# Projections in four parts, three and five per gap of a level; sums of squares' vector work in later gaps; a reordered head

## The reference

```python
qkvz = xn @ W_qkvz ; b, a = xn @ W_ba        # 16 heads of q and k, 32 of v and z, 128 wide
q, k, v = silu(causal_conv1d(qkv, 4 taps))
beta = sigmoid(b); g = -exp(A_log) * softplus(a + dt_bias)
q, k = rmsnorm(q), rmsnorm(k)                # from sums of squares over 128 channels
# chunks of 64 tokens: T = inverse(I + tril(beta k k^T * decay)), then 8 steps per sequence
# v_new = v' - k_cum @ state; out = q*exp(g) @ state + attn @ v_new; state = decayed state + k^T v_new
h = norm_w * rmsnorm(out) * silu(z)
s = h @ W_out
y = x + s * silu(ffn(xn))                    # ffn with weights looked up in a table of 16
```

## Time and profile before

| | us |
|---|---|
| three runs, median (lowest, highest) | 2787.88 (2787.59, 2792.42) |
| the profiled execution | 2787.02 |
| its span, first to last instruction | 2785.1 |
| round to round (start of `outputs`, 196.58 to 274.58) | 78.0 |
| PE busy (share of the span) | 2496.7 (90%) |
| DVE, ACT, POOL busy | 1660.4, 1492.5, 1802.1 |
| the chain that ended last, by engine | PE 68%, DVE 20%, no recorded cause 6%, the rest 6% |

### The profile page before, as it was taken

One profiled execution on the slowest core, in us unless ns is written; L12 is line 12 of the kernel. 1 busy time (PEld: TensorE's weight loads), 2 busy tenths in 40 slices (PEclk: granted clock), 3 DMA queues, 4 the chain that ended last, 5 costly groups with the idle time before them and its releaser, 6 DMA issues.

```text
span 2785.1 us, 104069 instructions
## 1 busy us (share of the span) xinstructions
PE 2496.7 (90%) x41680; PEld 1718.8 (62%) x41680; DVE 1660.4 (60%) x2967; ACT 1492.5 (54%) x3206; POOL 1802.1 (65%) x1829
## 2 busy tenths in 40 slices
PE   3599999989999998999999899999899999998799
PEld 1366666666666666666666566666666666666444
DVE  5466666666666666666666566666566666665322
ACT  1456566555556566555556566555565566554211
POOL 0576667787666666787666667787666667787100
PEclk8799999999999999999999999999999999998899
DMA  3111011111111011111111011011110111110200
GB/s 96 35 35 31 16 31 39 30 34 33 35 35 31 17 30 40 28 35 33 35 35 31 17 31 39 28 35 33 36 35 16 32 31 39 27 35 2 58 22 16
DMA packets 71100, 90.28 MB, mean 32 GB/s; under 512 B 16720, under 2 KB 39376, under 8 KB 70480
## 3 DMA queue, kind: packets, MB, share of 16 engines
q1 hardware_dynamic: 70608, 83.40, 11.7%
HBM read 78.30 MB, written 5.08 MB: 30 GB/s over the span
## 4 chain that ended last, share of the span: by engine, by line
PE 68%; DVE 20%; issue 6%; DVEq 1%; ACT 1%; DMA 0%; POOLq 0%; ACTq 0%; SPq 0%; POOL 0%
PE ps_two L406 9%; PE ps_two L582 8%; DVE XW L926 6%; PE ps_p L422 5%; PE ps_p L524 4%; PE ps_state L387 4%; PE ps_two L387 4%; PE ps_state L548 4%; DVE XW L937 4%; PE ps_p L419 3%; PE ps_p L418 3%; PE ps_p L502 3%; PE ps_two L572 3%; DVE hT L990 2%; PE ps_p L532 2%
## 5 line engine op out<-in xcount | busy, mean ns | idle before, releaser
L1072 POOL TENSOR_TENSOR Sd<-St,el 128x512 f32<-128x512 f32 x192 | 201.2, 1048 | 605.3 <-DVEq L971 500.1
L1108 POOL TENSOR_SCALAR hT<-idx_s,lutb 128x134 f32<-128x134 int32 x480 | 355.4, 744 | 27.5
L954 DVE TENSOR_SCALAR Vn<-ps_p,bR 128x128 f32<-128x128 f32 x512 | 164.6, 349 | 257.2 <-PE ps_p L497 183.6
L742 ACT ACTIVATE Xs<-XW 64x512 f32<-64x512 f32 x320 | 200.9, 628 | 207.7 <-DVE XW L937 201.5
L418 PEld LDWEIGHTS ps_p<-XW,U 64*64 64x64 f32 x5120 | 170.9, 137 | 222.3 <-issue 222.3
L857 DVE SCALAR_TENSOR_TENSOR cacc<-ps_two,cw,cacc 128x1022 f32<-128x1022 f32 (+2 forms) x192 | 243.1, 1266 | 84.2 <-ACT cacc L653 81.8
L418 PE MATMUL ps_p<-XW,U 64*64 64x64 f32 x5120 | 189.3, 223 | 112.0 <-DVE XW L926 104.2
L387 PE MATMUL ps_two<-xnT,w_qkv 128*128 128x512 f32 x512 | 258.7, 629 | 21.6 <-DVEq L862 19.8
L857 DVE SCALAR_TENSOR_TENSOR cacc<-ps_state,cw,cacc 128x1022 f32<-128x1022 f32 (+2 forms) x192 | 244.4, 1273 | 39.7 <-ACT cacc L653 18.2
L387 PE MATMUL ps_state<-xnT,w_qkv 128*128 128x512 f32 x512 | 253.3, 618 | 0.8 <-DVEq L862 0.8
L422 PEld LDWEIGHTS ps_p<-XW,P 64*64 64x64 f32 x5120 | 166.7, 136 | 132.1 <-issue 132.0
(11 more groups left out here) (156 smaller groups left out, 6115.5 us busy)
## 6 DMA issues: line engine op xcount, KB each, us to landing
qg<-g_scratch SPq DMA_DIRECT2D x64, 512.0 KB, 7.3
g_st<-g_scratch SPq DMA_DIRECT2D x64, 256.0 KB, 5.5
w_qkv<-in_wqkvz SPq DMA_DIRECT2D x16, 512.0 KB, 3.8
w_z<-in_wqkvz SPq DMA_DIRECT2D x16, 256.0 KB, 3.1
w_o<-in_wout SPq DMA_DIRECT2D x16, 256.0 KB, 2.8
idx_s<-in_idx SPq DMA_DIRECT2D x32, 67.0 KB, 1.9
fw_scratch<-looked_up SPq DMA_DIRECT2D x32, 67.0 KB, 1.9
Kg<-in_x SPq DMA_DIRECT2D x2, 1024.0 KB, 7.6
```

The costliest lines, as they stand in the source:

```text
L742: act.activation(Xs[(1 - a) * C:(2 - a) * C], X[a * C:(a + 1) * C, 1], ACT.Copy).then_inc(s["x_c"], 1)
L1072: pool.tensor_tensor(Sd[:, :, :, :], St[:, c % 2, :, :, :], el[:, R.par, :, :, c].unsqueeze(3).broadcast_to([P, BB, RATIO, P]), ALU.mult). ...
L1108: m = pool.tensor_scalar(slots[k], idx_s[:, :], float(k), lutb[:, k:k + 1], ALU.is_equal, ALU.mult)
```

## The change

`beside` cuts a projection into four parts (k = 0, 1 for columns 0 to 255, then for 256 to 511). The first gap of a level gets parts 0, 1, 2 of the level's first projection, the second gap its part 3 and all four of the next: three and five instead of four and four. DVE's `lengths` becomes three pieces: keys' copies in step 1, reciprocal and product in step 2, queries' copies in step 7, and POOL's `with_beta` goes to steps 3 and 4. In the head POOL normalises tiles 8 to 15; ACT copies every second bank of transposes; the head projections come in ahead of and between the turned gates; tap0 of kinds 0 and 1 goes first on ACT, and `decays(HEAD)` behind silu(1); SP loads the rows as soon as g is stored, and the scalars behind the second store; POOL's `lengths(HEAD)` goes behind `first_level`. Two small inputs of the head (`wba_s`, `resets`) lie in P1 instead of cacc.

```diff
--- before.py
+++ after.py
@@ -72,7 +72,7 @@
...
 IN_LAST, _ = places(bank_uses(False))
-IN_HEAD, PER_HEAD = places(spread(PROJ, (0, 1, 6, 7)) + spread(N2, (0, 1)))
+IN_HEAD, PER_HEAD = places(spread(PROJ, (6, 7, 0, 1)) + spread(N2, (2, 3)))
 def constants():
@@ -279,16 +279,23 @@
...
         sp.dma_start(w_z[:, :, :], wqkvz[:, :, bass.ds(h * HW + 4 * HD, 2 * HD)]).then_inc(s["ld_wz"], 16)
-    def load_round(h, par):
+    def load_scalars(h, par):
         b0 = par * BB
...
                          ).then_inc(s["ld_round"], 16)
...
+    def load_rows(h, par):
+        b0 = par * BB
         for a in range(RATIO):
...
             sp.dma_start(qg[:, par, :, a, :], src.broadcast_to([P, BB, S])).then_inc(s["ld_round"], 16)
...
+    def load_round(h, par):
+        load_scalars(h, par)
+        load_rows(h, par)
     def load_idx(h, par):
@@ -299,10 +306,12 @@
...
     sp.dma_start(g_dram.rearrange("b h t -> (b h) t"), gw[0]).then_inc(s["g_out"], 16)
+    sp.wait_ge(s["g_out"], 16)
+    load_rows(0, 0)
     sp.wait_ge(s["g_sc"], 8)
...
     sp.wait_ge(s["g_out"], 32)
-    load_round(0, 0)
+    load_scalars(0, 0)
     def body(R):
@@ -348,13 +357,14 @@
...
         if q >= 2:
-            pe.wait_ge(s["ln_T"], q - 1)
+            pe.wait_ge(s["ln_T"] if q % 2 == 0 else s["ln_Ta"], q // 2)
         for i in range(4):
             t, k = (q * 4 + i) // KD, (q * 4 + i) % KD
-            pe.wait_ge(s["ln_xn"], t + 1)
+            pe.wait_ge(s["ln_xn"] if t < NT // 2 else s["ln_xp"], t % (NT // 2) + 1)
             m = pe.transpose(ps[q % 2][:, i * P:(i + 1) * P], xn[t // 8][:, t % 8, k * P:(k + 1) * P], ident)
         m.then_inc(s["ln_t"], 1)
-    pe.wait_ge(s["ln_T"], NT * KD // 4)
+    pe.wait_ge(s["ln_T"], NT * KD // 8)
+    pe.wait_ge(s["ln_Ta"], NT * KD // 8)
     for j in range(2):
@@ -363,30 +373,34 @@
...
         m.then_inc(s["ba_mm"], 1)
-    for j, src in enumerate((bdup, gdup)):
+    def turn_gates(j, src):
         pe.wait_ge(s["g_dup"], j + 1)
...
         m.then_inc(s["g_tr"], 1)
-    pe.wait_ge(s["g_sc"], 8)
     pe.wait_ge(s["zeroed"], 1)
...
         return slice((par * BB + b) * S, (par * BB + b + 1) * S)
-    def proj(R, i):
+    def proj(R, i, parts=(0, 1, 2, 3)):
         par = 0 if R.head else 1 - R.par
         kind, b = i // BB, i % BB
-        if i == 0:
-            pe.wait_ge(s["ld_w"], 32 if R.head else (R.h + R.par) * 32 + 32)
-        bank, filled = wait_open(pe, R, "proj", i)
-        for k in range(KD):
-            m = pe.matmul(bank[:, :], w_qkv[:, k, kind * P:(kind + 1) * P], xnT[:, k, cols(par, b)],
+        bank, filled = ps[R.use("proj", i)[0]], full[R.use("proj", i)[0]]
+        if 0 in parts:
+            if i == 0:
+                pe.wait_ge(s["ld_w"], 32 if R.head else (R.h + R.par) * 32 + 32)
+            wait_open(pe, R, "proj", i)
+        for part in parts:
+            k, t0 = part % KD, part // KD * (S // 2)
+            rows = xnT[:, k, (par * BB + b) * S + t0:(par * BB + b) * S + t0 + S // 2]
+            m = pe.matmul(bank[:, t0:t0 + S // 2], w_qkv[:, k, kind * P:(kind + 1) * P], rows,
                           start=(k == 0), stop=(k == KD - 1))
-        m.then_inc(filled, 1)
+        if 3 in parts:
+            m.then_inc(filled, 1)
     def lengths(R, i):
@@ -465,8 +479,11 @@
...
         if lv < 5:
-            if R.nxt:
-                proj(R, PROJ_AT[lv][half])
+            if R.nxt and half == 0:
+                proj(R, PROJ_AT[lv][0], (0, 1, 2))
+            elif R.nxt:
+                proj(R, PROJ_AT[lv][0], (3,))
+                proj(R, PROJ_AT[lv][1])
         elif half == 0:
@@ -583,8 +600,17 @@
...
             m.then_inc(filled, 1)
-    for i in range(8):
+    for i in range(2):
         proj(HEAD, i)
+    turn_gates(0, bdup)
+    pe.wait_ge(s["ba_act"], 1)
+    pe.wait_ge(s["g_c"], 1)
+    for i in range(2, 4):
+        proj(HEAD, i)
+    turn_gates(1, gdup)
+    for i in range(4, 8):
+        proj(HEAD, i)
+    pe.wait_ge(s["g_sc"], 8)
     for i in range(2):
@@ -633,6 +659,11 @@
...
         act.activation(std[:, t:t + 1], mv[:, t, 1:2], ACT.Sqrt, bias=eps[:, 0:1]).then_inc(s["ln_std"], 1)
+    for q in range(1, NT * KD // 4, 2):
+        act.wait_ge(s["ln_t"], q + 1)
+        dst = xnT[:, :, q * 2 * P:(q + 1) * 2 * P].rearrange("p k (t i) -> p t k i", i=P)
+        act.activation(dst, ps[q % 2][:, :].rearrange("p (t k i) -> p t k i", t=2, k=KD), ACT.Copy
+                       ).then_inc(s["ln_Ta"], 1)
     act.wait_ge(s["ba_mm"], 2)
@@ -685,10 +716,14 @@
...
             act.activation(qg[:, par, b, :, :], qg[:, par, b, :, :], ACT.Exp).then_inc(s["dec_act"], 1)
-    decays(HEAD)
+    tap0(HEAD, 0)
+    tap0(HEAD, 1)
     for kind in range(4):
-        tap0(HEAD, kind)
         silu(HEAD, kind)
+        if kind < 2:
+            tap0(HEAD, kind + 2)
+        if kind == 1:
+            decays(HEAD)
     def gate(R, i):
@@ -792,11 +827,11 @@
...
         dve.reciprocal(rstd[:, t:t + 1], std[:, t:t + 1]).then_inc(s["ln_inv"], 1)
-    for t in range(NT):
+    for t in range(NT // 2):
         dve.wait_ge(s["ln_inv"], t + 1)
...
                           ALU.subtract, ALU.mult).then_inc(s["ln_xn"], 1)
-    for q in range(NT * KD // 4):
+    for q in range(0, NT * KD // 4, 2):
         dve.wait_ge(s["ln_t"], q + 1)
@@ -870,25 +905,35 @@
...
                                   ).then_inc(s["n2_c"], 1)
-    def lengths(R):
+    def key_sums(R):
...
+        bank, done = wait_full(dve, R, "n2", 1)
+        sums(bank, kn[:, :, :], 1.0, HD * RMS_EPS)
+        dve.wait_ge(s["n2_c"], R.at(4, 10, 10))
+        dve.sem_inc(done, 1)
...
+    def key_scales(R):
...
+        par = 0 if R.head else 1 - R.par
+        dve.wait_ge(s["n2_c"], R.at(4, 10, 10))
+        dve.reciprocal(rk2[:, :, :], kn[:, :, :]).then_inc(s["n2_c"], 1)
+        dve.wait_ge(s["n2_c"], R.at(5, 10, 10))
+        dve.wait_ge(s["ld_round"], R.at(96, 96, 96))
+        dve.tensor_tensor(bR[:, par], rk2[:, :, :], sc[:, par, 1], ALU.mult).then_inc(s["n2_c"], 1)
...
+    def query_sums(R):
         par = 0 if R.head else 1 - R.par
...
         sums(bank, eqs[:, par], HD * RMS_EPS, (HD * RMS_EPS) ** 2)
-        dve.wait_ge(s["n2_c"], R.at(4, 10, 10))
+        dve.wait_ge(s["n2_c"], R.at(10, 10, 10))
         dve.sem_inc(done, 1)
-        bank, done = wait_full(dve, R, "n2", 1)
-        sums(bank, kn[:, :, :], 1.0, HD * RMS_EPS)
-        dve.wait_ge(s["n2_c"], R.at(8, 10, 10))
-        dve.sem_inc(done, 1)
-        dve.reciprocal(rk2[:, :, :], kn[:, :, :]).then_inc(s["n2_c"], 1)
-        dve.wait_ge(s["n2_c"], R.at(9, 10, 10))
-        dve.wait_ge(s["ld_round"], R.at(96, 96, 96))
-        dve.tensor_tensor(bR[:, par], rk2[:, :, :], sc[:, par, 1], ALU.mult).then_inc(s["n2_c"], 1)
     for kind in range(4):
         taps(HEAD, kind, (1, 2, 3))
-    lengths(HEAD)
+    key_sums(HEAD)
+    key_scales(HEAD)
+    query_sums(HEAD)
     def per_chunk(t, n):
@@ -957,6 +1002,10 @@
...
                 gated(R, GATE_AT[c])
+            if c == 1 and R.nxt:
+                key_sums(R)
+            if c == 2 and R.nxt:
+                key_scales(R)
             if c < NC - 1:
@@ -969,8 +1018,8 @@
...
                 dve.sem_inc(done, 1)
-            if c == 0 and R.nxt:
-                lengths(R)
+            elif R.nxt:
+                query_sums(R)
     def scale_o(R, i):
@@ -1033,6 +1082,10 @@
...
     pool.wait_ge(s["ld_const"], 16 * n_const)
+    for t in range(NT // 2, NT):
+        pool.wait_ge(s["ln_inv"], t + 1)
+        pool.tensor_scalar(xn[t // 8][:, t % 8, :], x_in[t // 8][:, t % 8, :], mv[:, t, 0:1], rstd[:, t:t + 1],
+                           ALU.subtract, ALU.mult).then_inc(s["ln_xp"], 1)
     def decay(R):
@@ -1055,7 +1108,7 @@
...
         pool.wait_ge(s["dec_act"], R.at(2 * b + 1, 4, 4))
-        pool.wait_ge(s["n2_c"], R.at(10, 10, 10))
+        pool.wait_ge(s["n2_c"], R.at(6, 10, 10))
         pool.tensor_tensor(DB[:, b, :, :], Dm[:, b, :, :], bR[:, par, b, :].unsqueeze(2).broadcast_to([P, NC, C]),
@@ -1084,11 +1137,13 @@
...
     def lengths(R):
-        pool.wait_ge(s["n2_c"], R.at(8, 10, 10))
+        pool.wait_ge(s["n2_c"], R.at(4, 10, 10))
         pool.tensor_tensor(rinv[:, :, :], kn[:, :, :], eps[:, 3:4].unsqueeze(2).broadcast_to([P, BB, NC]),
...
     def norm(R, i):
+        if i == 0:
+            pool.wait_ge(s["n2_c"], R.at(0, 10, 10))
         pool.wait_ge(s["o_sq"], R.at(i + 1, 0, 4))
@@ -1138,11 +1193,11 @@
...
     decay(HEAD)
-    lengths(HEAD)
     for b in range(BB):
...
         first_level(HEAD, b)
+    lengths(HEAD)
     scale_q(HEAD, 0)
@@ -1155,8 +1210,8 @@
...
                 norm(R, c // 2 - 1)
-            if R.nxt and c in (1, 3):
-                with_beta(R, c // 2)
+            if R.nxt and c in (3, 4):
+                with_beta(R, c - 3)
             elif R.nxt and c > 4:
```

## The result

The changed kernel runs in **2699.91 us** (median of four runs, 2697.78 to 2702.26), where the kernel before beside it took 2787.74 (2786.09 to 2792.42): ratio 0.9677, 95% interval 0.9665 to 0.9688, 88 us less. The profiled execution took 2698.88 us with a span of 2697.0.

A forecast was written before the change was run, and what follows sets the result against it. PE held 68% of the chain of waits and DVE 20%. Savings of 30.1 (levels), 36.3 (recurrence) and 32.0 (head) sum to 98.4 us, taking 2787.0 to 2689 us, range 2672 to 2720.

The forecast's parts named there:

- Part A: Level gaps: projections split three and five parts save 0.97 us a round, 30.1 in 31 rounds.
- The floor is 1.29, so the whole 0.43 counts, with 0.23 over: First gap of a level: p2 cannot start sooner than 1.29 us after p1's end, so 1.52 is reachable.
- so 0.36 of 0.86 is left: Level 4: ACT's chain lets p2 start no earlier than 227.02 against 227.38, leaving 0.36 us for levels 3 and 4.
- the second gap had room: Second gap of a level: the extra 0.43 us part fits in PE's 0.61 idle before p1, 0.18 over.
- Part B: Recurrence: moving the small vector work out of step 1's way saves 1.17 us a round, 36.3 in all.
- POOL's cover: Recurrence step 5: Sd, 0.37 us later behind `with_beta`, still ends before St, with 0.16 over.
- Part C: Head, once: reordered work up to the first p1 saves 32.0 us, bounds 26 to 35.
- the layer norm's 1.0: Head: giving POOL eight layer norm tiles of 256 columns gains 1.0 us.
- Slower by unhidden loads: Rival, level gaps: extra weight loads of 256-column matmuls show; 3040 us if not hidden at all; chance 0.03.
- A gives all: Rival, levels: ACT's chain is less rigid, the split gives 1.72 us a round, 2666 us; chance 0.07.
- B gives half: Rival, recurrence: St waits for keys' copies or Sd for POOL, 0.6 us a round, 2706 us; chance 0.12.
- A gives nothing: Rival, levels: thin covers at DVE's taps and the second gap fail, levels keep 6.73 us, 2719 us; chance 0.15.

The follow-up runs named there:

- the run: Changed kernel with the head of before and the rounds as changed: 2733.09 us, 33.2 more than the changed kernel.
- the quarters run: Changed kernel with projections still cut in four parts, but four parts in each gap instead of three and five: 2711.92 us, 12.0 more than the changed kernel.

## Why the prediction was right, and where not

**Part A, wrong in size: 0.97 forecast, 0.40 measured, below its bounds of 0.5 to 1.72.** The step that failed is "The floor is 1.29, so the whole 0.43 counts, with 0.23 over". That floor is 0.12 from p1's end to the copy and 1.17 from there to p2, and the 1.17 was read in the last round, where targets are constants. In the loop of the changed kernel p1 ends at 171.12 and p2 starts at 172.79: the floor is 0.13 + 1.03 + 0.51 = 1.67, above the 1.52 that the gap was cut down to. Undoing the split, reordering the waits and dropping one settle it. So the first gaps of levels 1 to 3 gave 0.16 to 0.18 each, and level 4, whose copy is fixed by ACT's chain, lost 0.16. I had a row that could have warned me. Level 4 of the loop had 227.38 - 226.87 = 0.51 between copy's end and p2, but I took that as slack ("so 0.36 of 0.86 is left") when it was the floor.

The rest of A held. Cutting cost nothing, ACT's chain was anchored at level 3, and the second gap had room: the wait ahead of p1 shrank from 104.2 us to 46.0 over the kernel. Behind the loop, where the floor is as it was read, the split gave 1.00. With the waits in the right order, split and order are worth 29.9, the forecast's 30.1 for the split alone; the order by itself has 7.9 of it, so this is no proof of the sum.

The total came within 11 us because A is under a third of it: 17.8 missing there, 3.1 and 1.2 over in B and C, and 3 more that no single part has.

**Part B, right: 1.17 forecast, 1.27 measured** (39.4 us for 36.3). The lines that answer to the earlier trace rows:

```profile
212.89 0.64 PE L541 MATMUL ps_p<-St,Kg 128*64 128x128 f32 x8
213.90 0.71 PE L565 MATMUL ps_state<-Vn,Kd 64*128 64x128 f32 x8
215.43 0.77 PE L541 MATMUL ps_p<-St,Kg 128*64 128x128 f32 x8 [0.22 <-DVE St L1018]
...
213.36 0.61 DVE L999 TENSOR_SCALAR Vn<-ps_p,bR 128x128 f32<-128x128 f32 x2 [1.15 <-PE ps_p L541]
213.88 0.75 DVE L905 TENSOR_SCALAR kn<-ps_two 64x8 f32<-64x8 f32 x4
214.95 0.75 DVE L1018 TENSOR_TENSOR St<-Sd,ps_state 128x256 f32<-128x256 f32 x2 [0.32 <-DVE kn L905]
...
223.13 1.04 POOL L1112 TENSOR_TENSOR DB<-Dm,bR 128x512 f32<-128x512 f32 x1
224.13 1.05 POOL L1125 TENSOR_TENSOR Sd<-St,el 128x512 f32<-128x512 f32 x1
225.40 0.75 DVE L1018 TENSOR_TENSOR St<-Sd,ps_state 128x256 f32<-128x256 f32 x2 [0.24 <-PE ps_state L565]
```

Vn waits for PE and no longer for DVE's own sums: step 1's L565, the state's part, starts at 213.90, 1.01 behind L541, where the kernel before had 2.44 (246.79 to 249.23). That is 1.43 gained for 1.31 forecast. The keys' copies do end the wait of step 1's St, as feared: from L565 to the next L541 it is 1.53 (to 215.43) for 1.37, so they cost 0.16 for 0.14. Sd of step 5 follows `with_beta` at once and ends at 225.18, before St: St's wait ends on PE, so POOL's cover held.

**Part C, right: 32.0 forecast, 33.2 by the run, 32.4 by the trace.** Head rows, answering to the earlier trace rows:

```profile
20.37 10.03 POOL L1087 TENSOR_SCALAR hT<-Kd,kq 128x256 f32<-128x256 f32 x8 [16.13 <-DVE kq L829]
31.67 3.68 PE L372 MATMUL ps_two<-xnT,P 128*32 128x512 f32 x32 [0.78 <-ACT xnT L665]
54.47 3.91 DVE L892 SCALAR_TENSOR_TENSOR cacc<-ps_state,cw,cacc 128x1022 f32<-128x1022 f32 x3
58.49 5.93 PE L400 MATMUL ps_state<-xnT,w_qkv 128*128 128x256 f32 x16 [5.88 <-DVEq L897]
77.74 3.78 PE L450 MATMUL ps_p<-kq 128*128 128x128 f32 x16 [7.07 <-ACT vs L698]
80.07 0.43 DVE L953 SCALAR_TENSOR_TENSOR U<-ps_p,DB 128x256 f32<-128x256 f32 x1 [3.96 <-POOL DB L1117]
90.81 0.34 PE L432 MATMUL ps_p<-XW,U 64*64 64x64 f32 x1 [3.01 <-ACT V L752]
```

kkq came 28.7 earlier (forecast 27.3, the layer norm's 1.0 in it), U 34.7 earlier, the first p1 32.4: beyond U 2.3 was lost again, and the first p1 waited for ACT's V last. Behind kkq 3.7 came for the 4.7 forecast. So the single terms were off by 0.5 to 1.5 us in both directions and met in the sum. The layer norm's 1.0 was 0.5 in the trace (gate matmuls at 31.67 for 32.21) and nothing that the times can tell. Here POOL took 10.03 / 8 = 1.25 for 128x256, where DVE took 0.39 (3.12 / 8) beside it and 0.33 (2.66 / 8) alone. By the Trainium skill (GPSIMD Engine Reference, section 4.1) the two engines should be close for such an operation; the trace disagrees by a factor of over three, and the forecast was right to lean on its row.

**Rivals.** Slower by unhidden loads: refuted by the quarters run. A gives all: refuted. By the time alone, 2700 us, "B gives half" (2706) would have looked nearest; undoing B showed that it gave all, and that A had fallen short. "A gives nothing" (2719) pointed at the right part, for reasons (DVE's taps, the second gap) that were not the cause.

## What to carry to other kernels

A distance read where the loop is unrolled is not that of the loop: check a floor in the rounds it will bind. Ahead of a critical instruction, put the waits that were met long ago first and the one that ends last at the end, since each target worked out from a loop register costs an instruction. The sequencer's records in a trace show where these stand; dropping a wait can move one to a worse place. Undo the parts of a change one at a time: here the total hid that one part gave less than half. And a stall can have two prices, its own length and the clock behind it.

## What was not expected of the hardware

- A register instruction behind the wait that ends last costs TensorE 0.09 us on the path (records at 172.31, 172.40, 172.50, 172.59 and 172.68): 0.51 to 0.57 against 0.14 from ACT's copy to p2, and 0.10 a level when one moved. On DVE the order gained 0.08 in one step and lost 0.05 and 0.08 in two others.
- The same stall was followed by the lower clock in some rounds only: 15 of 31 for stalls of 2.0 to 2.4 us without a matmul, 2 of 31 for one of 1.36 in the kernel before, none of 31 for one of 1.28. What decides it in a given round stays open.
- DVE's layer norm took 0.39 us an operation while POOL worked beside it, 0.33 alone.
